# Mixture-of-experts stage of a two-layer decoder: gathered tokens turned on TensorE, or by strip transfers and VectorE's 32 by 32 transposes

## Chip, cores and metric

One core of one Trainium2 chip runs the whole program. The metric is device time in microseconds (us), lower is better. The kernel before takes 2111.92 us, the median of 3 runs (2110.97 to 2113.27).

## What is computed

Two decoder layers over 8 sequences of 256 tokens with 512 features, everything in float32: differential attention, a long convolution, a mixture of experts (MoE), local attention, cross attention and a gated attention, with a residual and a layer norm behind each. Only the MoE matters here. Every token picks 2 of 8 experts, and the stage computes for each pick

```
h = silu(x @ gate[e]) * (x @ up[e])      # x: 512 features, h: 352
y = h @ down[e]                          # y: 512 features
```

The two results are then weighted by the router's shares and summed.

## The kernel before

Stages follow each other with a barrier of all engines between them: front, long convolution, middle (layer norm, router, sorting of the picks into tiles), experts, tail. The middle stage sorts the 4096 picks by expert into `TILES` = 39 tiles of 128 tokens, one expert each, and keeps for each tile its list of tokens (`tokens`) and its expert (`tile_expert`).

`experts_stage` (from L1593) handles the tiles in order, s = 0 to 38. For each tile:

- GpSimd (L1620) gathers 128 rows of x from HBM into `xg[s % 2]` by an indirect DMA, once TensorE has turned the tile that lay there.
- TensorE turns the rows (`turn_x`, L1634): four 128x128 transposes into one PSUM bank, `xT_ps`. VectorE copies the bank to SBUF as `xT` (L1716). Features now lie on partitions.
- TensorE computes gate and up (`project`, L1639), four matmuls each, into `gu_ps`. ScalarE takes silu of gate (L1690), VectorE multiplies by up (L1721), TensorE turns the hidden rows (L1658), ScalarE copies them (L1705, L1707), and TensorE multiplies by the down matrix (`moe_y_ps`, L1667).
- VectorE copies y to SBUF (L1733), and ScalarE's queue stores it in HBM (L1694).

The order of TensorE's work is written out by hand: gate of tile s+1, turn of the hidden rows of s, up of s+1, turn of x of s+2, down of s. The expert of a tile is a number in SBUF, which TensorE's sequencer reads (L1626, `TENSOR_LOAD`) behind the semaphore waits and ahead of the matmuls. VectorE's order in each step is product of s+1, copy of the turned x of s+2, copy of y of s. SyncE (SP) has nothing to do in this stage. ScalarE's queue issues at the start a 1 MB load, `early_wq`, which the tail uses.

The tail turns some of its own blocks another way (`turn_strips`, L188, and `shift_strips`, L194): VectorE's transposes turn each 32 by 32 block in its place, and 16 DMAs, one for each pair of a source strip of 32 partitions and a target strip, carry the blocks to their partitions. In each such DMA 32 partitions send 8 runs of 32 floats:

```
eng.dma_start(out.rearrange("p c (t q) -> p (c t) q", q=P)[lanes, :, rows],
              blocks.rearrange("p (n k) -> p n k", k=P)[rows, :, lanes]).then_inc(done, 16)
```

Of the kernel before, what the change touches and what calls it, by code (L numbers as in the profile page):

```python
# [193 lines left out]
def shift_strips(eng, out, blocks, done):  # L194


    for s in range(4):
        for k in range(4):
            lanes, rows = slice(32 * k, 32 * k + 32), slice(32 * s, 32 * s + 32)
            eng.dma_start(out.rearrange("p c (t q) -> p (c t) q", q=P)[lanes, :, rows],  # L200
                          blocks.rearrange("p (n k) -> p n k", k=P)[rows, :, lanes]).then_inc(done, 16)


def project_cols(pe, out, w, xT, col, n=P):
# [965 lines left out]
def ctx_stores(b):  # L1170

    return sum(2 if n >= EARLY else 1 for n in range(b % 2, b, 2))
# [420 lines left out]
def experts_stage(nc, consts, mid, region, x_in, y_slots, early, early_loaded, w_tail):  # L1593


    with ExitStack() as ctx:
        st = Stage(nc, ctx, "moe")
        at = AT_SMALL + 320 + 4 * D
        xT = mid.xT
        hT = region.at("moe_hT", at + 2048, [P, 3, P])  # L1600
        y = [region.at(f"moe_y{p}", at + 3584 + 2048 * p, [P, D]) for p in range(2)]
        silu = region.at("moe_silu", AT_CTX + 2 * KB4, [P, 2, HID])
        hid = region.at("moe_hid", AT_CTX + 2 * KB4 + 2816, [P, 2, HID])
        xg, wgu, wd, gathered = mid.xg, mid.gu, mid.down, mid.gathered
        gu_ps = st.ps("gu_ps", [P, 2, 2, 512])
        xT_ps = st.ps("xT_ps", [P, 512])
        hT_ps = st.ps("hT_ps", [P, 512])
        y_ps = st.ps("y_ps", [P, 2, 512])
        y_stored = mid.y_stored
        sem = {n: st.sem(n) for n in (  # L1610
            "x_turned", "xT_taken", "gate_ready", "up_ready", "silu_ready", "hid_ready", "h_turned", "hT_taken", "y_ready", "y_taken")}

        with nc.Block() as block:
            @block.gpsimd
            def _(pool):
                for s in range(2, TILES):
                    p = s % 2
                    if s > 2:
                        pool.wait_ge(sem["x_turned"], s - 2)
                    pool.indirect_dma_start(out=xg[p][:], out_offset=None, in_=x_in,  # L1620
                                            in_offset=bass.IndirectOffsetOnAxis(ap=mid.tokens[:, s:s + 1], axis=0)).then_inc(gathered[p], 16)

            @block.tensor
            def _(pe):
                def expert(s):
                    return pe.value_load(mid.tile_expert[0:1, s:s + 1], min_val=0, max_val=E_ - 1)  # L1626

                def turn_x(s):
                    p = s % 2
                    pe.wait_ge(gathered[p], 16 * (s // 2) + 16)  # L1630
                    if s > 1:
                        pe.wait_ge(sem["xT_taken"], s - 1)
                    for c in range(NC):
                        ins = pe.transpose(xT_ps[:, c * P:(c + 1) * P], xg[p][:, c * P:(c + 1) * P], consts["ident"][:])  # L1634
                    ins.then_inc(sem["x_turned"], 1)

                def project(s, h, e):
                    for c in range(NC):
                        ins = pe.matmul(gu_ps[:, s % 2, h, 0:HID], (xT if s else mid.xT_first)[:, c, :], wgu[c][:, e, h * HID:(h + 1) * HID],  # L1639
                                        start=c == 0, stop=c == NC - 1)  # L1640
                    return ins

                def gate(s):
                    if s:
                        pe.wait_ge(sem["xT_taken"], s)
                    if s >= 2:
                        pe.wait_ge(sem["hid_ready"], s - 1)
                    project(s, 0, expert(s)).then_inc(sem["gate_ready"], 1)

                def up(s):  # L1650
                    project(s, 1, expert(s)).then_inc(sem["up_ready"], 1)

                def turn_hid(s):
                    pe.wait_ge(sem["hid_ready"], s + 1)
                    if s:
                        pe.wait_ge(sem["hT_taken"], s)
                    for n, (lo, w) in enumerate(HC):
                        ins = pe.transpose(hT_ps[0:w, n * P:(n + 1) * P], hid[:, s % 2, lo:lo + w], consts["ident"][:])  # L1658
                    ins.then_inc(sem["h_turned"], 1)

                def down(s):
                    e = expert(s)
                    pe.wait_ge(sem["hT_taken"], s + 1)
                    if s >= 2:
                        pe.wait_ge(sem["y_taken"], s - 1)
                    for n, (lo, w) in enumerate(HC):
                        ins = pe.matmul(y_ps[:, s % 2, :], hT[0:w, n, :], wd[n][0:w, e, :], start=n == 0, stop=n == 2)  # L1667
                    ins.then_inc(sem["y_ready"], 1)

                pe.wait_ge(mid.first_half, 16 * 7)  # L1670
                gate(0)
                turn_x(1)
                up(0)
                for s in range(TILES):
                    if s + 1 == HALVES[1][0]:
                        pe.wait_ge(mid.second_half, 16 * 6)
                    if s + 1 < TILES:
                        gate(s + 1)
                    turn_hid(s)
                    if s + 1 < TILES:  # L1680
                        up(s + 1)
                    if s + 2 < TILES:
                        turn_x(s + 2)
                    down(s)

            @block.scalar
            def _(act):
                def swish(s):
                    act.wait_ge(sem["gate_ready"], s + 1)
                    act.activation(silu[:, s % 2, :], gu_ps[:, s % 2, 0, 0:HID], ACT.Silu).then_inc(sem["silu_ready"], 1)  # L1690

                def store(s):
                    act.wait_ge(sem["y_taken"], s + 1)
                    act.dma_start(y_slots[s * P:(s + 1) * P, :], y[s % 2][:]).then_inc(y_stored[s % 2], 16)  # L1694

                for p in range(2):
                    act.wait_ge(mid.ctx_stored[p], 16 * ctx_stores(B - 2 + p))
                for k in early:
                    act.dma_start(early[k][:], w_tail[k].rearrange("(c p) e -> p c e", p=P)).then_inc(early_loaded[k], 16)
                swish(0)  # L1700
                for s in range(TILES):
                    if s + 1 < TILES:
                        swish(s + 1)
                    act.wait_ge(sem["h_turned"], s + 1)
                    act.copy(hT[:, 0:2, :], hT_ps[:, 0:2 * P].rearrange("p (k n) -> p k n", n=P))  # L1705
                    w = HC[2][1]
                    act.copy(hT[0:w, 2, :], hT_ps[0:w, 2 * P:3 * P]).then_inc(sem["hT_taken"], 1)  # L1707
                    if s:
                        store(s - 1)
                store(TILES - 1)  # L1710

            @block.vector
            def _(dve):
                def take_x(s):
                    dve.wait_ge(sem["x_turned"], s)
                    dve.tensor_copy(xT[:], xT_ps[:].rearrange("p (c n) -> p c n", n=P)).then_inc(sem["xT_taken"], 1)  # L1716

                def product(s):
                    dve.wait_ge(sem["silu_ready"], s + 1)
                    dve.wait_ge(sem["up_ready"], s + 1)  # L1720
                    dve.tensor_tensor(hid[:, s % 2, :], gu_ps[:, s % 2, 1, 0:HID], silu[:, s % 2, :], ALU.mult).then_inc(sem["hid_ready"], 1)  # L1721

                take_x(1)
                product(0)
                for s in range(TILES):
                    if s + 1 < TILES:
                        product(s + 1)
                    if s + 2 < TILES:
                        take_x(s + 2)
                    dve.wait_ge(sem["y_ready"], s + 1)  # L1730
                    if s >= 2:
                        dve.wait_ge(y_stored[s % 2], 16 * (s // 2))
                    dve.tensor_copy(y[s % 2][:], y_ps[:, s % 2, :]).then_inc(sem["y_taken"], 1)  # L1733


def tail_stage(nc, consts, region, y_stored, x_in, x_out, y_slots, slot, share, ctx_q, ctx_o, wa, wvo, w, early, early_loaded, cT, ctx_wq, ctx_wo):
# [5 lines left out]
    with ExitStack() as ctx:  # L1742
# [124 lines left out]
        with nc.Block() as block:  # L1867
# [412 lines left out]
            def _(sp):  # L2280
# [17 lines left out]
                def shift(k, b, key):  # L2298
                    sp.wait_ge(blocks_made[k], blocks_count(k, b))
                    sp.wait_ge(ring.filled_sem(key), ring.count(key))  # L2300
                    shift_strips(sp, xT[b % 2][:], blocks_of(k), xT_loaded[b % 2])

                for r in range(B + 3):
                    if 2 <= r < B:
# [736 lines left out]
```

## Time and profile before

| What | Value |
|---|---|
| Median of 3 runs | 2111.92 us |
| Profiled execution | 2113.61 us |
| Its span | 2111.7 us |
| TensorE matmuls busy | 2041.3 us (97%) |
| VectorE busy | 1146.7 us (54%) |
| ScalarE, GpSimd busy | 500.7 us, 579.5 us |
| Granted TensorE clock, mean | 0.993 of full speed |

A row of the trace names the line of the program, the engine, the operation and the tiles (out<-in). PE is TensorE's matmuls, PEld its weight loads, DVE VectorE, ACT ScalarE, POOL GpSimd, and SPq, ACTq and POOLq are the queues on which SyncE, ScalarE and GpSimd issue DMAs. A float32 matmul has two records, so four matmuls show as x8; a transpose has one. Duration of a matmul is longer than the distance to the next, since they are pipelined: distances are taken from start to start.

### The profile page before, as it was taken

The page shows a single profiled execution, that of the slowest core. Times are in us where ns is not written, and L with a number is a line of the kernel's source. Part 1 is how long each engine was busy: PE and PEld are TensorE (multiplying, and loading weights), DVE is VectorE, ACT ScalarE, POOL GpSimd, SP SyncE. Part 2 cuts the span into 40 slices and gives each one's busy share as a digit, 9 for nine tenths or more (in the row PEclk, how much of TensorE's full clock was granted, in tenths as well). Part 3 has the DMA queues.
Part 4 walks back from the last instruction along what each step waited for, and adds up shares of the span by engine and source line. Part 5 has one row for each costly group of instructions (what it writes and reads, how often), then busy time and mean ns, then how long its engine had stood idle before and what let it go on. Part 6 is the DMA issues. An engine that isn't in the chain of part 4 may idle for free. (4 is left out here: it accounts for less than half of the span.)

```text
span 2111.7 us, 32316 instructions
## 1 busy us (share of the span) xinstructions
PE 2041.3 (97%) x13303; PEld 1180.7 (56%) x13303; DVE 1146.7 (54%) x1748; ACT 500.7 (24%) x757; POOL 579.5 (27%) x548
## 2 busy tenths in 40 slices
PE   7899999999999999999999999999999999999996
PEld 5444444334444467556565665656666666666664
DVE  2567777576777764122222234365757474736567
ACT  2445444440000131111111122112222222222211
POOL 2122222228999710011111322112222212121112
PEclk9999999999999999999999999999999999999998
DMA  5101111206111146422221502302030302020000
GB/s 161 49 1 56 56 56 46 88 27 219 42 40 44 32 168 224 172 65 65 65 65 60 209 21 91 80 12 70 11 81 11 81 11 61 8 54 11 1 11 21
DMA packets 140222, 139.74 MB, mean 66 GB/s; under 512 B 80464, under 2 KB 93904, under 8 KB 140080
## 3 DMA queue, kind: packets, MB, share of 16 engines
q1 hardware_dynamic: 119952, 86.42, 13.7%
q10 hardware_dynamic: 14448, 32.64, 4.3%
q0 software_dynamic: 5680, 18.62, 3.0%
q8 instruction: 110, 1.80, 0.4%
q14 instruction: 32, 0.26, 0.0%
HBM read 97.40 MB, written 41.81 MB: 66 GB/s over the span
## 5 line engine op out<-in xcount | busy, mean ns | idle before, releaser
L1049 PE MATMUL conv_conv<-kv,toep 128*128 128x512 f32 x576 | 247.5, 593 | 0.0
L2659 DVE RECIPROCAL tail_inv<-tail_ring 128x256 f32<-128x256 f32 x63 | 110.7, 1756 | 172.4 <-PE tail_ring L1971 171.8
L1639 PE MATMUL moe_gu_ps<-gu,xT_tile 128*128 x608 | 192.4, 459 | 0.0
L1049 PEld LDWEIGHTS conv_conv<-kv,toep 128*128 128x128 f32 x576 | 109.9, 191 | 138.2 <-issue 131.0
L1083 POOL TENSOR_TENSOR kv<-vT,cT 128x512 f32<-128x512 f32 x128 | 147.1, 1173 | 16.9 <-PE conv_conv L1049 13.1
L2344 POOL TENSOR_TENSOR tail_rstd_x<-tail_rstd_x,const_minus_half 128x2 f32<-128x2 f32 x31 | 21.7, 700 | 468.4 <-DVE tail_rstd_x L2617 468.4
L1639 PEld LDWEIGHTS moe_gu_ps<-gu,xT_tile 128*128 128x128 f32 x608 | 112.5, 190 | 66.3 <-issue 17.8
L2352 POOL TENSOR_SCALAR_AFFINE_SELECT tail_expT<-tail_expT 128x1024 f32<-128x1024 f32 x64 | 71.3, 1116 | 227.6 <-ACT tail_expT L2436 227.4
L2647 DVE TENSOR_REDUCE tail_negtop<-tail_scores 128x4 f32<-128x1024 f32 x64 | 77.9, 1218 | 82.6 <-PE tail_scores L1922 82.5
L610 POOL TENSOR_SCALAR_AFFINE_SELECT front_expT<-front_expT 128x2048 f32<-128x2048 f32 x32 | 64.1, 2004 | 199.6 <-ACT front_expT L665 199.6
L1721 DVE TENSOR_TENSOR moe_hid<-moe_gu_ps,moe_silu 128x352 f32<-128x352 f32 x39 | 20.4, 524 | 170.7 <-PE moe_gu_ps L1639 170.7
L1620 POOL DMA_INDIRECT xg<-x_after,tokens x37 | 35.0, 945 | 282.2 <-PE moe_xT_ps L1634 255.1
L665 ACT ACTIVATE front_expT<-front_scores 128x2048 f32<-128x2048 f32 x48 | 90.1, 1878 | 78.2 <-PE front_scores L383 78.2
L1667 PE MATMUL moe_y_ps<-down,moe_hT 128*128 (+1 forms) x234 | 107.1, 593 | 0.7 <-ACT moe_hT L1707 0.7
L2436 ACT ACTIVATE tail_expT<-tail_scores 128x1536 f32<-128x1536 f32 x63 | 91.4, 1450 | 65.1 <-PE tail_scores L1948 65.1
L786 DVE TENSOR_REDUCE front_negtop<-front_scores 128x8 f32<-128x2048 f32 x32 | 73.2, 2288 | 22.1 <-PE front_scores L351 21.9
L1690 ACT ACTIVATE moe_silu<-moe_gu_ps 128x352 f32<-128x352 f32 x39 | 18.1, 463 | 270.3 <-PE moe_gu_ps L1639 270.3
L2357 POOL TENSOR_TENSOR tail_expT<-tail_expT 128x512 f32<-128x512 f32 x60 | 76.7, 1278 | 5.0
L1105 ACT COPY both<-conv_conv 128x512 f32<-128x512 f32 x32 | 18.6, 585 | 229.4 <-PE conv_conv L1049 212.0
L1733 DVE COPY moe_y<-moe_y_ps 128x512 f32<-128x512 f32 x39 | 27.0, 691 | 72.7 <-PE moe_y_ps L1667 72.7
L214 PE MATMUL tail_ring<-tail_gk,tail_xT 128*128 128x416 f32 (+1 forms) x256 | 63.0, 398 | 0.8 <-ACT tail_xT L2418 0.8
L1667 PEld LDWEIGHTS moe_y_ps<-down,moe_hT 128*128 128x128 f32 (+1 forms) x234 | 41.6, 191 | 38.4 <-issue 38.2
(396 smaller groups left out, 3879.9 us busy)
## 6 DMA issues: line engine op xcount, KB each, us to landing
toep<-toeplitz SPq DMA_DIRECT2D x32, 320.0 KB, 2.9
y_slots<-moe_y ACTq DMA_DIRECT2D x39, 256.0 KB, 2.0
gu<-in_L_ffn_gate_up_proj SPq DMA_DIRECT2D x5, 1408.0 KB, 12.4
toeplitz<-filt_rows SPq DMA_DIRECT2D x8, 768.0 KB
tail_xT<-tail_probs SPq DMA_DIRECT2D x176, 32.0 KB
front_e<-in_ctx SPq DMA_DIRECT2D x8, 512.0 KB, 9.7
toeplitz<-filt_rows SPq DMA_DIRECT2D x16, 256.0 KB
x_after<-x SPq DMA_DIRECT2D x8, 512.0 KB, 5.0
```

What stands on the lines that cost most here:

```text
L610: pool.affine_select(out=tile, in_=tile, compare_op=ALU.is_ge, fill=0.0, base=0, pattern=[[0, 16], [1, P]], channel_multiplier=-1).then_in ...
L665: act.activation(exp_buf(b, n)[:].rearrange("p g j q -> p g (j q)"), scores[:], ACT.Exp).then_inc(quads.drained_sem(key), 1)
L786: ins = dve.tensor_reduce(negtop[:, 1, n].rearrange("p (g a) -> p g a", a=2), scores[:].rearrange("p g (a k) -> p g a k", a=2), AX_X, ALU. ...
L1049: ins = pe.matmul(bank, toep[p][:, mat * P:(mat + 1) * P], kv[p][:, c].rearrange("p b j i -> p (b j i)"), start=n == 0, stop=n == len(PART ...
L1083: pool.tensor_tensor(kv[p][:, c], tokens_of(c, h), context_of(c, h, 3), ALU.mult).then_inc(kv_ready, 1)
L1639: ins = pe.matmul(gu_ps[:, s % 2, h, 0:HID], (xT if s else mid.xT_first)[:, c, :], wgu[c][:, e, h * HID:(h + 1) * HID], start=c == 0, stop ...
L1667: ins = pe.matmul(y_ps[:, s % 2, :], hT[0:w, n, :], wd[n][0:w, e, :], start=n == 0, stop=n == 2)
L2352: pool.affine_select(out=diagonal, in_=diagonal, compare_op=ALU.is_ge, fill=0.0, base=0, pattern=[[0, 8], [1, P]], channel_multiplier=-1). ...
L2357: pool.tensor_tensor(e[:, 3], e[:, 0], e[:, 2], ALU.add).then_inc(masked[kind], 1)
L2436: act.activation(exp_buf(kind, b, c)[:, 0:3].rearrange("p n g q -> p g n q"), quads.tile(key)[:, :, 0:3 * P].rearrange("p g (n q) -> p g n ...
L2647: dve.tensor_reduce(negtop[:, 1, heads_of(c)], scores[:, :, 0:S], AX_X, ALU.max, negate=True)
L2659: link.after(dve.reciprocal(inv[c % 2][:], bank[:, S:2 * S]))
```

## The change

The x of tiles 2 to 38 is no longer turned by TensorE. GpSimd gathers two tiles (2q and 2q+1) into one of two pair buffers. SyncE, once both have landed and VectorE has made `xT` of tile 2q-1, issues the 16 strip DMAs of `shift_strips` from the pair buffer to the one buffer `shifted`. VectorE turns the 32 by 32 blocks of one tile at a time from `shifted` into `xT[s % 2]` (`make_xT`). The copy from PSUM by VectorE and TensorE's four transposes are gone for these tiles; tile 1 keeps them. `xT` has two buffers now. The load `early_wq` moves from the stage's start to the step ahead of the last tile, since a pair buffer lies at its place. `shift_strips` itself takes flat arguments, which changes nothing for the tail.

```diff
 def shift_strips(eng, out, blocks, done):
+    to, of = (a.rearrange("p (n q) -> p n q", q=P) for a in (out, blocks))
     for s in range(4):
         for k in range(4):
             lanes, rows = slice(32 * k, 32 * k + 32), slice(32 * s, 32 * s + 32)
...
+            eng.dma_start(to[lanes, :, rows], of[rows, :, lanes]).then_inc(done, 16)
@@ experts_stage
-        xT = mid.xT
+        pairs = [region.at(f"moe_pair{n}", AT_CTX + n * KB4, [P, 2, D]) for n in range(2)]
+        shifted = region.at("moe_shifted", AT_SMALL + 320, [P, 2, D])
+        xT = [region.at("moe_xT0", AT_RAW + GU_BYTES, [P, NC, P]), region.at("moe_xT1", AT_CTX + 2 * KB4 + 5632, [P, NC, P])]
...
             @block.gpsimd
             def _(pool):
                 for s in range(2, TILES):
-                    p = s % 2
-                    if s > 2:
-                        pool.wait_ge(sem["x_turned"], s - 2)
-                    pool.indirect_dma_start(out=xg[p][:], out_offset=None, in_=x_in,
+                    q, t = s // 2, s % 2
+                    if q < 3 and t == 0:
+                        pool.wait_ge(mid.ctx_stored[q - 1], 16 * ctx_stores(B - 3 + q))
+                    elif t == 0:
+                        pool.wait_ge(sem["x_shifted"], 256 * (q - 2))
+                    pool.indirect_dma_start(out=pairs[(q - 1) % 2][:, t], out_offset=None, in_=x_in,
...
+            @block.sync
+            def _(sp):
+                for q in range(1, PAIRS + 1):
+                    tiles = range(2 * q, min(2 * q + 2, TILES))
+                    sp.wait_ge(paired[q % 2], 16 * sum(1 for s in range(2, tiles[-1] + 1) if s // 2 % 2 == q % 2))
+                    sp.wait_ge(sem["xT_made"], 2 * q - 1)
+                    shift_strips(sp, shifted[:, 0:len(tiles)].rearrange("p t d -> p (t d)"),
+                                 pairs[(q - 1) % 2][:, 0:len(tiles)].rearrange("p t d -> p (t d)"), sem["x_shifted"])
...
                 def gate(s):
                     if s:
-                        pe.wait_ge(sem["xT_taken"], s)
+                        pe.wait_ge(sem["xT_made"], s)
...
                     if s + 1 < TILES:
                         up(s + 1)
-                    if s + 2 < TILES:
-                        turn_x(s + 2)
                     down(s)
...
-                for k in early:
-                    act.dma_start(early[k][:], w_tail[k].rearrange("(c p) e -> p c e", p=P)).then_inc(early_loaded[k], 16)
                 swish(0)
                 for s in range(TILES):
                     if s + 1 < TILES:
                         swish(s + 1)
+                    if s + 2 == TILES:
+                        act.wait_ge(sem["x_shifted"], 256 * PAIRS)
+                        for k in early:
+                            act.dma_start(early[k][:], w_tail[k].rearrange("(c p) e -> p c e", p=P)).then_inc(early_loaded[k], 16)
...
             @block.vector
             def _(dve):
-                def take_x(s):
-                    dve.wait_ge(sem["x_turned"], s)
-                    dve.tensor_copy(xT[:], xT_ps[:].rearrange("p (c n) -> p c n", n=P)).then_inc(sem["xT_taken"], 1)
+                def make_xT(s):
+                    dve.wait_ge(sem["x_shifted"], 256 * (s // 2))
+                    if s > 2:
+                        dve.wait_ge(sem["up_ready"], s - 1)
+                    dve.transpose(xT[s % 2][:].rearrange("p c n -> p (c n)"), shifted[:, s % 2]).then_inc(sem["xT_made"], 1)
...
-                take_x(1)
+                dve.wait_ge(mid.ctx_stored[1], 16 * ctx_stores(B - 1))
+                dve.wait_ge(sem["x_turned"], 1)
+                dve.tensor_copy(xT[1][:], xT_ps[:].rearrange("p (c n) -> p c n", n=P)).then_inc(sem["xT_made"], 1)
```

The order of instructions on TensorE, ahead of the down matmuls of one tile and the gate of the next. Before:

```order
 L1639 MATMUL moe_gu_ps<-gu_67,xT_tile 128x352
 L1634 MATMUL moe_xT_ps<-const_ident,xg_75 128x128 [waits moe_xT_taken,mid_gathered0]
 L1634 MATMUL moe_xT_ps<-const_ident,xg_75 128x128 x3
 L1626 TENSOR_LOAD tile_expert
 L1626 ISA x2
 L1667 ISA [waits moe_y_taken,moe_hT_taken]
 L1667 MATMUL moe_y_ps<-down_68,moe_hT 128x512
```

With the change, from the down matmuls to the next gate:

```order
 L1642 TENSOR_LOAD tile_expert
 L1642 ISA x2
 L1680 ISA [waits moe_y_taken,moe_hT_taken]
 L1680 MATMUL moe_y_ps<-down_68,moe_hT 128x512
 L1680 REGISTER_ALU
 L1680 MATMUL moe_y_ps<-down_69,moe_hT 128x512
 L1680 REGISTER_ALU
 L1680 MATMUL moe_y_ps<-down_70,moe_hT 128x512
 L1642 TENSOR_LOAD tile_expert [waits moe_hid_ready,moe_xT_made]
 L1642 ISA x2
 L1652 ISA
 L1652 MATMUL moe_gu_ps<-gu_64,moe_xT_7468 128x352
```

The four transposes between up and down are gone, and the gate's read of the expert's number stands behind a wait for `xT_made`.

On SyncE's queue, behind the stage's barrier, where there was nothing before (two of the 19 pairs):

```order
 L1630 UNCONDITIONAL_BRANCH [waits barrier_Pool_Activation_PE_DVE_SP_release]
 L201 DMA moe_shifted<-moe_pair_7464 32x8x32 [waits moe_xT_made,moe_paired1]
 L201 DMA moe_shifted<-moe_pair_7464 32x8x32 x15
 L201 DMA moe_shifted<-moe_pair_7465 32x8x32 [waits moe_xT_made,moe_paired0]
 L201 DMA moe_shifted<-moe_pair_7465 32x8x32 x15
```

And on VectorE, in the steady state:

```order
 L1736 TENSOR_TENSOR moe_hid<-moe_gu_ps,moe_silu 128x352 [waits moe_up_ready,moe_silu_ready]
 L1731 STREAM_TRANSPOSE moe_xT_7468<-moe_shifted 128x512 [waits moe_up_ready,moe_x_shifted]
 L1750 COPY moe_y_7470<-moe_y_ps 128x512 [waits mid_y_stored0,moe_y_ready]
 L1736 TENSOR_TENSOR moe_hid<-moe_gu_ps,moe_silu 128x352 [waits moe_up_ready,moe_silu_ready]
 L1731 STREAM_TRANSPOSE moe_xT_7467<-moe_shifted 128x512 [waits moe_up_ready,moe_x_shifted]
```

The 32x8x32 DMAs are new on SyncE, 16 for each pair behind a wait for `xT_made`; on VectorE the transpose has the place of the copy `xT_tile<-moe_xT_ps`, behind the product and ahead of the copy of y.

## Rows read from the trace of the kernel before

**Rows 1.** The page: span, busy time, and its 40 slices.
```profile
span 2111.7 us, 32316 instructions
PE 2041.3 (97%) x13303; PEld 1180.7 (56%) x13303; DVE 1146.7 (54%) x1748; ACT 500.7 (24%) x757; POOL 579.5 (27%) x548
...
PE   7899999999999999999999999999999999999996
```

**Rows 2.** Stretches: us, busy PE, PEld, DVE, ACT, POOL; clock, DMA share, GB/s.
```profile
859.00:1180.00 321.00, 316.94 (x1127) 189.62 (x1127) 70.17 (x116) 35.94 (x118) 34.96 (x37) 0.99 0.21 69
1010.44:1018.52 8.08, 8.08 (x30) 4.85 (x29) 1.81 (x3) 0.89 (x3) 0.94 (x1) 1.00 0.21 67
```

**Rows 3.** Timeline of one tile, TensorE and VectorE: start, us, what.
```profile
1002.36 0.60 PE L1634 MATMUL moe_xT_ps<-const_ident,xg 128*128 128x128 f32 x4
...
1002.63 0.52 DVE L1721 TENSOR_TENSOR moe_hid<-moe_gu_ps,moe_silu 128x352 f32<-128x352 f32 x1 [4.44 <-PE moe_gu_ps L1639]
...
1002.80 2.74 PE L1667 MATMUL moe_y_ps<-down,moe_hT 128*128 x6
1003.07 0.68 DVE L1716 COPY xT_tile<-moe_xT_ps 128x512 f32<-128x512 f32 x1
...
1005.38 2.53 PE L1639 MATMUL moe_gu_ps<-gu,xT_tile 128*128 x8
...
1007.75 0.49 PE L1658 MATMUL moe_hT_ps<-const_ident,moe_hid 128*128 128x128 f32 x3
...
1008.07 2.53 PE L1639 MATMUL moe_gu_ps<-gu,xT_tile 128*128 x8
...
1010.44 0.60 PE L1634 MATMUL moe_xT_ps<-const_ident,xg 128*128 128x128 f32 x4
```

**Rows 4.** The instructions on the tile moe_xT_ps (ns min/median/max).
```profile
L1634 PE MATMUL moe_xT_ps<-const_ident,xg x152: 272/273/273, 865.2 to 1164.3; 128*128 128x128 f32 x152
```

**Rows 5.** Timeline of SyncE's queue in the tail: trains of 16 strip DMAs.
```profile
1336.18 10.98 SPq L200 DMA_DIRECT2D tail_xT<-tail_probs  x16
1351.30 10.38 SPq L200 DMA_DIRECT2D tail_xT<-tail_probT  x16
...
1538.39 11.78 SPq L200 DMA_DIRECT2D tail_xT<-tail_probs  x16
...
1884.44 11.28 SPq L200 DMA_DIRECT2D tail_xT<-tail_probT  x16
```

**Rows 6.** The tile tail_xT: its strip DMAs, ns to issue one.
```profile
L200 SPq DMA_DIRECT2D tail_xT<-tail_probs x176: 585/611/1607, 1336.2 to 1874.5; - x176
```

**Rows 7.** Stretches around the train of 1351.30 (last two numbers: DMA share, GB/s).
```profile
1351.30:1352.30 1.00, 1.00 (x3) 0.38 (x2) 0.00 (x0) 0.54 (x1) 0.00 (x0) 1.00 0.00 0
1352.30:1361.50 9.20, 9.20 (x41) 5.37 (x40) 0.00 (x0) 1.17 (x2) 0.00 (x0) 1.00 0.31 50
...
1362.40:1362.70 0.30, 0.30 (x13) 0.18 (x6) 0.00 (x0) 0.00 (x0) 0.00 (x0) 1.00 0.56 90
1362.70:1363.00 0.30, 0.30 (x2) 0.27 (x3) 0.28 (x1) 0.00 (x0) 0.00 (x0) 1.00 0.00 0
```

**Rows 8.** Line L191: VectorE's transposes in the tail.
```profile
L191 DVE STREAM_TRANSPOSE tail_probs<-tail_x x11: 1233/1245/1245, 1334.9 to 1862.5; 128x1024 f32<-128x1024 f32 x11
```

**Rows 9.** Line L1626: what TensorE's sequencer does for an expert's number.
```profile
L1626 PEldq TENSOR_LOAD <-tile_expert x117: 295/302/1499, 859.1 to 1172.9; - x117
L1626 PEldq FUSED_REGOPS  x117: 151/151/165, 860.6 to 1173.3; - x117
```

**Rows 10.** Timeline at the start of the stage: TensorE, VectorE, ScalarE's wait.
```profile
861.03 4.32 PE L1639 MATMUL moe_gu_ps<-gu,xT_first 128*128 x8 [4.00 <-issue]
...
864.78 1.28 ACT L1690 ACT_TABLE_LOAD   x1 [7.12 <-DMA ctx_o<-ctxo]
...
865.19 0.60 PE L1634 MATMUL moe_xT_ps<-const_ident,xg 128*128 128x128 f32 x4
...
865.83 0.69 DVE L1716 COPY xT_tile<-moe_xT_ps 128x512 f32<-128x512 f32 x1 [14.93 <-PE moe_xT_ps L1634]
```

**Rows 11.** Stretches with idle TensorE ahead of work at a low clock.
```profile
393.00:396.80 3.80, 0.00 (x0) 0.00 (x0) 3.53 (x5) 1.02 (x1) 2.55 (x2) 1.00 0.73 245
396.80:400.20 3.40, 3.18 (x4) 1.31 (x5) 0.00 (x0) 0.00 (x0) 0.00 (x0) 0.58 0.28 106
...
857.00:861.00 4.00, 0.04 (x1) 0.00 (x0) 0.00 (x0) 0.59 (x1) 0.94 (x1) 1.00 0.56 136
861.00:864.50 3.50, 3.47 (x7) 2.10 (x8) 0.00 (x0) 0.00 (x0) 0.00 (x0) 0.58 0.88 299
```

**Rows 12.** The page: DMA issues, KB each, us to landing.
```profile
y_slots<-moe_y ACTq DMA_DIRECT2D x39, 256.0 KB, 2.0
...
early_wq<-in_L_attn_w_qkv ACTq DMA_DIRECT2D x1, 1024.0 KB, 5.3
...
xg<-x_after,tokens POOLq DMA_INDIRECT x39, 3.3
```

More of the change, by code:

```diff
@@ L199, in shift_strips @@
             lanes, rows = slice(32 * k, 32 * k + 32), slice(32 * s, 32 * s + 32)
-            eng.dma_start(out.rearrange("p c (t q) -> p (c t) q", q=P)[lanes, :, rows],
-                          blocks.rearrange("p (n k) -> p n k", k=P)[rows, :, lanes]).then_inc(done, 16)
+            eng.dma_start(to[lanes, :, rows], of[rows, :, lanes]).then_inc(done, 16)
 def project_cols(pe, out, w, xT, col, n=P):
@@ L1610, in experts_stage @@
         sem = {n: st.sem(n) for n in (
-            "x_turned", "xT_taken", "gate_ready", "up_ready", "silu_ready", "hid_ready", "h_turned", "hT_taken", "y_ready", "y_taken")}
+            "x_turned", "x_shifted", "xT_made", "gate_ready", "up_ready", "silu_ready", "hid_ready", "h_turned", "hT_taken", "y_ready", "y_taken")}
+        paired = [st.sem(f"paired{p}") for p in range(2)]
+        PAIRS = (TILES - 1) // 2
         with nc.Block() as block:
@@ L1616, in _ @@
                 for s in range(2, TILES):
-                    p = s % 2
-                    if s > 2:
-                        pool.wait_ge(sem["x_turned"], s - 2)
-                    pool.indirect_dma_start(out=xg[p][:], out_offset=None, in_=x_in,
-                                            in_offset=bass.IndirectOffsetOnAxis(ap=mid.tokens[:, s:s + 1], axis=0)).then_inc(gathered[p], 16)
+                    q, t = s // 2, s % 2
[4 more added lines that the diff above has]
+                    pool.indirect_dma_start(out=pairs[(q - 1) % 2][:, t], out_offset=None, in_=x_in,
+                                            in_offset=bass.IndirectOffsetOnAxis(ap=mid.tokens[:, s:s + 1], axis=0)).then_inc(paired[q % 2], 16)
+            @block.sync
[6 more added lines that the diff above has]
+                                 pairs[(q - 1) % 2][:, 0:len(tiles)].rearrange("p t d -> p (t d)"), sem["x_shifted"])
             @block.tensor
@@ L1626, in expert, with turn_second @@
                     return pe.value_load(mid.tile_expert[0:1, s:s + 1], min_val=0, max_val=E_ - 1)
[L1628 to L1632, printed above, removed]
+                def turn_second():
+                    pe.wait_ge(gathered[1], 16)
                     for c in range(NC):
-                        ins = pe.transpose(xT_ps[:, c * P:(c + 1) * P], xg[p][:, c * P:(c + 1) * P], consts["ident"][:])
+                        ins = pe.transpose(xT_ps[:, c * P:(c + 1) * P], xg[1][:, c * P:(c + 1) * P], consts["ident"][:])
                     ins.then_inc(sem["x_turned"], 1)
@@ L1638, in project @@
                     for c in range(NC):
-                        ins = pe.matmul(gu_ps[:, s % 2, h, 0:HID], (xT if s else mid.xT_first)[:, c, :], wgu[c][:, e, h * HID:(h + 1) * HID],
+                        ins = pe.matmul(gu_ps[:, s % 2, h, 0:HID], (xT[s % 2] if s else mid.xT_first)[:, c, :], wgu[c][:, e, h * HID:(h + 1) * HID],
                                         start=c == 0, stop=c == NC - 1)
@@ L1671, in _ @@
                 gate(0)
-                turn_x(1)
+                turn_second()
                 up(0)
@@ L1728, in _ @@
                     if s + 2 < TILES:
-                        take_x(s + 2)
+                        make_xT(s + 2)
                     dve.wait_ge(sem["y_ready"], s + 1)
@@ L2300, in shift @@
                     sp.wait_ge(ring.filled_sem(key), ring.count(key))
-                    shift_strips(sp, xT[b % 2][:], blocks_of(k), xT_loaded[b % 2])
+                    shift_strips(sp, xT[b % 2][:].rearrange("p c s -> p (c s)"), blocks_of(k), xT_loaded[b % 2])
                 for r in range(B + 3):
```

## Prediction

> **What bounds the kernel now.** I read the page first, then the stage's own stretch, then one tile's timeline. TensorE is busy 97% of the span [rows 1], so any other engine matters only where TensorE waits for it. The experts' stage is the stretch from 859 to 1180 us: 316.94 of 321.00 us of it are matmuls, at a clock of 0.99 [rows 2]. Inside, a tile takes 8.08 us with 8.08 us of TensorE busy [rows 2]; no engine and no DMA is waited for. The period can be read off the starts in [rows 3]: turn of x 0.44 us (1002.36 to 1002.80), down 2.58, gate 2.37, turn of the hidden rows 0.32, up 2.37, sum 8.08. Whatever leaves TensorE shortens the program one for one, and whatever TensorE then waits for lengthens it.
>
> **What the change removes.** There are 152 transposes in 38 turns [rows 4]; one turn stays. 37 x 0.44 = **16.3 us** leave TensorE. VectorE loses 37 copies of 0.68 us [rows 3] and gets 37 transposes of 128x512. The tail's transposes of 128x1024 take 1.245 us [rows 8], so half of that, 0.62 us, is my estimate; by the nearest copy it would be 0.68. In either case VectorE has room (1.81 us busy of 8.08 [rows 2]).
>
> **What it adds: a serial loop through SyncE.** `shifted` has one buffer. The 16 strip DMAs of pair q start only when `xT` of tile 2q-1 is made, and `xT` of tile 2q needs all 16 to have landed. TensorE works meanwhile, but only on what it already has. So I compare two paths, both from T, the end of up of tile 2q-2 (1002.36 in [rows 3]), to the first gate matmul of tile 2q.
>
> TensorE's own work: down 2.58, gate of 2q-1 2.37, turn of hidden rows 0.32, up of 2q-1 2.37, down 2.58 = **10.22 us**.
>
> The loop:
> - Product starts at T+0.27 and takes 0.52 [rows 3]; the transpose of tile 2q-1 follows: xT made at T+1.4.
> - SyncE issues 16 DMAs. The same helper with the same shape (32 partitions x 8 runs of 128 bytes, 32 KB) runs in the tail 17 times: the trains take 10.38 to 11.78 us, mean 11.0 [rows 5], and one issue takes 0.611 us in the median, 0.585 at least [rows 6]. It is the queue's issuing that takes the time, not the moving: while the train of 1351.30 runs, the DMA engines are 0.31 busy at 50 GB/s [rows 7]. I take 11.0, since one store of y falls in each train here, as loads do in some of the tail's.
> - Landing: that train's last issue ended at 1361.68, and the DMA share falls to nothing at 1362.70 [rows 7]: 1.0 us, with semaphores 1.2.
> - Transpose of tile 2q: 0.6.
> - TensorE's sequencer was waiting, so its read of the expert's number is no longer covered by running matmuls: 0.30 + 0.15 [rows 9], some register work and the first weights. The read took 1.5 us the one time it stood behind a barrier [rows 9]. Bounds 0.4 and 1.9; I take 0.9, near the median read.
>
> Sum 1.4 + 11.0 + 1.2 + 0.6 + 0.9 = 15.1 us, against 10.22: TensorE **waits 4.9 us in every pair**. After it the pair goes on with gate, turn and up, and the next loop starts; nothing makes up for the wait, because each train begins behind the one before's last reader. The first pair is the same: its train waits for the copy of tile 1 (from 865.83 [rows 10]), 13.7 us ahead of gate 2, which TensorE could start at 875.6.
>
> There are 19 trains, 18 of full size: 18 x 4.9 = **88.2 us**. The last carries one tile, 16 DMAs of half the bytes: no row shows such an issue; between a full train (4.9) and a wait of 0, I take 2.
>
> **The clock.** An idle TensorE is followed by a low clock in this trace. After 3.80 us without a matmul the clock of the next 3.40 us was 0.58, after 4.00 us idle it was 0.58 for 3.50 us [rows 11], that is at the lower level, 1.2 GHz. The gate that followed took 4.16 us (861.03 to 865.19 [rows 10]) in place of 2.37: 1.8 us lost. A wait of 4.9 us is longer than both. Part of a low stretch may fall into the wait itself, where it costs nothing, so bounds 0 and 1.8 us for each wait; I take 1.3, nearer the upper, which both rows show: 19 x 1.3 = **24.7 us**.
>
> **What is hidden.** The indirect gathers stay as many, 0.94 us each on GpSimd, and land in 3.3 [rows 12]; a pair buffer is free when its own train has landed, a whole pair ahead. The y copy of tile 2q-2 now waits behind VectorE's blocked transpose, some 2 us later than before, but its bank is wanted again only after two more gates. VectorE's new wait for a context store ends when ScalarE's did, at 864.78, ahead of the turn it waits for at 865.19 [rows 10]. `early_wq` lands in 5.3 us [rows 12] with the last tile's up and two downs still to come: nothing.
>
> **Sum**, against the profiled execution: 2113.6 - 16.3 + 88.2 + 2 + 24.7 = 2212.2. That execution is 1.7 us over the median, so **2210.5 us**, 98.6 more than 2111.9. A measurement of this kernel can tell about 0.2%, 4 us.
>
> **A rule against the rows.** The sum prices a transfer by the time its queue takes to issue it [rows 5, 6]. The Trainium skill ("DMA: Bandwidth & Descriptors", section "Issuing engines are not separate DMA queues") says the opposite of what decides here: the sequencer's time to initiate a DMA is usually small relative to the DMA itself. By its fit of 2.0 us plus bytes over 436 GB/s, 512 KB would be shifted in some 3.2 us (an estimate from that page). The trace disagrees: 0.61 us of issue for each 32 KB. Were it so here, rival 1 would hold.
>
> **Rivals.**
> 1. *The trains hide and the change is faster.* TensorE waits for nothing if the train takes less than 10.22 - 1.4 - 1.2 - 0.6 - 0.9 = 6.1 us, that is 0.38 us for each issue. Then 2111.9 - 16.3 = 2095.6 us. For it: SyncE has nothing else in this stage, while in the tail it has loads beside. Against it: all 17 trains are above 10.3 us, quiet ones too, and the shortest of 176 issues was 0.585 us [rows 6]. 4%.
> 2. *The waits are there, the clock stays up.* The low stretches fall in the waits, or do not come. 2210.5 - 24.7 = 2185.8 us. For it: nothing in the rows says that a low stretch must begin only when TensorE resumes. Against: in both places of [rows 11] it did. 22%.
> 3. *The trains are longer here*, since y stores and gathers run beside them, or the expert's read takes 1.5 us each time. One issue took 1.607 us at most [rows 6]. With trains of 11.8, the read at its upper bound and the full clock loss, each wait is 6.7 + 1.8 us: 2111.9 - 16.3 + 18 x 8.5 + 6.7 = 2255 us, and beyond where trains pass 12 us. 8%.
>
> My forecast has 66%: waits near 4.9 with some clock loss, 2190 to 2245. **Range:** with trains of 10.4 us and the read at 0.4 a wait is 3.8, and without any clock loss that gives 2111.9 - 16.3 + 18 x 3.8 = 2164. I take 2165 to 2248, which leaves out rival 1, most of rival 3 and a little of the forecast's edges. **Chances:** slower by over 0.2% 0.95 (the forecast, rivals 2 and 3, short of a point for a train just short enough), faster 0.04, within 0.2% 0.01.
>
> **What would show it.** On SyncE's queue in this stage: 19 trains of 16, each near 11 us, starting some 0.05 us after a VectorE transpose of an odd tile. In TensorE's waits: 19 on the gate, near 4.9 us each, released by VectorE's transpose; pair period near 21 us instead of 16.2. Odd tiles' gates should wait for nothing. TensorE's clock in the stage below 0.99, with gates of even tiles near 3.7 us rather than 2.4. Transposes near 0.62 us. Wrong would be: trains under 6 us (rival 1), or a wait whose releaser is the gather or a y store.

## The result and the profile after

| | Before | Changed |
|---|---|---|
| Median | 2112.18 us (4 runs) | 2230.86 us (4 runs, 2228.03 to 2233.34) |
| Ratio | 1 | 1.0558, 95% interval 1.0543 to 1.0573 |
| Span of the profiled execution | 2111.7 us | 2225.6 us |
| Mean granted clock | 0.993 | 0.971 |

The change costs 118.7 us, 5.6%. The forecast was 2210.5 us in a range of 2165 to 2248.

The page of the changed kernel, against [rows 1] (the clock's row stands here too):

```profile
span 2225.6 us, 32343 instructions
...
PE 2070.6 (93%) x13155; PEld 1188.7 (53%) x13155; DVE 1148.3 (52%) x1748; ACT 502.0 (23%) x757; POOL 579.4 (26%) x548
...
PE   7899999999999998787878799999999999999996
...
PEclk9999999999999998888888899999999999999998
```

TensorE has fewer instructions (148 transposes are gone) and yet more busy time, and its share and its clock both fall in the slices of the experts' stage. The tail is untouched: from its first matmul (1294.46) to the end it takes 931.1 us, as before (from 1180.65, 931.0 us). The profiled execution reached the stage's first gate 6.2 us sooner (854.85 against 861.03 [rows 10]), in stages that the change leaves alone. So its span is 113.9 us longer, while the stage itself takes 120.0 us more. Two of the four runs of the changed kernel lie at 2228 us and two at 2233, and what makes this difference is not shown.

TensorE's waits in the stage (engine, line, released by: us in total, times, longest):

```profile
PE moe_gu_ps L1652 <- DVE moe_xT L1731: 82.0, 18, 5.3
PE moe_gu_ps L1652 <- issue: 8.2, 2, 4.4
```

The second row is one wait of the same kind (4.4 us) and the 3.8 us ahead of the stage's first gate, which stood there before as 4.0 [rows 10]. So the change adds 19 waits, 86.4 us, 4.55 each, all on a gate, all behind VectorE's transpose. Such a row counts from the end of the matmul before, which lies 0.16 us behind the start that the next one could have had (a down takes 2.74 us as a duration and 2.58 from start to start). So a wait costs 0.16 us more than listed: 4.71 in the mean, 89.5 us in all. What VectorE and SyncE waited for:

```profile
DVE moe_xT L1731 <- DMA moe_shifted<-moe_pair: 94.1, 19, 5.8
...
SPq L1635 <- DVE moe_xT L1731: 210.6, 18, 12.4
```

The loop can be read from these: TensorE waits for VectorE, VectorE for the strip transfers, and SyncE for VectorE's transpose of the tile before. Its pieces, from the timeline and from the rows of the tile `moe_shifted`:

```profile
997.16 10.40 SPq L201 DMA_DIRECT2D moe_shifted<-moe_pair  x16
...
1264.53 10.61 SPq L201 DMA_DIRECT2D moe_shifted<-moe_pair  x16
...
L201 SPq DMA_DIRECT2D moe_shifted<-moe_pair x304: 585/611/1605, 861.5 to 1274.5; - x152
L1731 DVE STREAM_TRANSPOSE moe_xT<-moe_shifted x37: 700/711/714, 874.0 to 1276.4; 128x512 f32<-128x512 f32 x37
...
DMA to landing us min/median/max: 1.8/1.9/3.2
```

Twelve of the 19 trains take 10.4 us, the others up to 11.4, and the mean is 10.6. An issue takes 0.611 us, as in the tail [rows 6]. The train at 1264.53 is the last, which moves one tile: half the bytes, and it takes no less. One pair on TensorE and VectorE:

```profile
1003.32 2.74 PE L1680 MATMUL moe_y_ps<-down,moe_hT 128*128 x6
1003.59 0.53 DVE L1736 TENSOR_TENSOR moe_hid<-moe_gu_ps,moe_silu 128x352 f32<-128x352 f32 x1 [4.44 <-PE moe_gu_ps L1652]
1008.87 0.71 DVE L1731 STREAM_TRANSPOSE moe_xT<-moe_shifted 128x512 f32<-128x512 f32 x1 [4.75 <-DMA moe_shifted<-moe_pair]
...
1010.39 4.32 PE L1652 MATMUL moe_gu_ps<-gu,moe_xT 128*128 x8 [4.34 <-DVE moe_xT L1731]
1014.55 0.49 PE L1671 MATMUL moe_hT_ps<-const_ident,moe_hid 128*128 128x128 f32 x3
...
1017.25 2.74 PE L1680 MATMUL moe_y_ps<-down,moe_hT 128*128 x6
1017.52 0.52 DVE L1736 TENSOR_TENSOR moe_hid<-moe_gu_ps,moe_silu 128x352 f32<-128x352 f32 x1 [7.36 <-PE moe_gu_ps L1652]
1017.96 0.70 DVE L1731 STREAM_TRANSPOSE moe_xT<-moe_shifted 128x512 f32<-128x512 f32 x1
1019.83 2.53 PE L1652 MATMUL moe_gu_ps<-gu,moe_xT 128*128 x8
```

The gate of the even tile starts 4.49 us late, counted from where down's 2.58 us end (1005.90), and then takes 4.16 us (1010.39 to 1014.55) instead of 2.37. The gate of the odd tile waits for nothing. This is the milder case: in 8 of the 19 even tiles the gate takes 3.9 to 4.2 us, in the other 11 it takes 4.85, and there the low clock reaches into the turn of the hidden rows, as behind the first and the last wait:

```profile
875.53 5.05 PE L1652 MATMUL moe_gu_ps<-gu,moe_xT 128*128 x8 [4.89 <-DVE moe_xT L1731]
880.38 0.73 PE L1671 MATMUL moe_hT_ps<-const_ident,moe_hid 128*128 128x128 f32 x3
...
1277.96 5.06 PE L1652 MATMUL moe_gu_ps<-gu,moe_xT 128*128 x8 [4.53 <-DVE moe_xT L1731]
1282.81 0.85 PE L1671 MATMUL moe_hT_ps<-const_ident,moe_hid 128*128 128x128 f32 x3
```

From 875.53 to 1277.96 there are 18 pairs: 22.36 us each, where two tiles took 16.16 before. The stretches of the pair above (us; busy PE, PEld, DVE, ACT, POOL; clock, DMA share, GB/s):

```profile
1005.90:1010.39 4.49, 0.16 (x1) 0.00 (x1) 1.29 (x2) 0.00 (x0) 0.98 (x2) 1.00 0.18 29
1010.39:1014.55 4.16, 4.16 (x8) 2.39 (x9) 0.00 (x0) 0.00 (x0) 0.91 (x1) 0.59 0.47 126
1014.55:1026.00 11.45, 11.45 (x40) 6.88 (x39) 2.36 (x4) 1.77 (x6) 0.00 (x0) 1.00 0.30 74
```

While TensorE waits, the DMA engines are 0.18 busy. The wait is a chain, one link after the other: SyncE still issues its last DMAs (to 1007.56, 1.7 us), they land (1.3 us, to 1008.87), VectorE transposes (0.7 us), TensorE starts (0.8 us).

Where the low clock begins differs between the two cases. The first wait, with its long stretch, and the wait of 1010.39, with a short one:

```profile
871.00:874.00 3.00, 0.00 (x0) 0.00 (x0) 0.00 (x0) 0.00 (x0) 0.00 (x0) 1.00 0.28 45
874.00:875.53 1.53, 0.00 (x1) 0.01 (x1) 1.29 (x2) 0.00 (x0) 0.95 (x2) 0.51 0.00 0
875.53:880.80 5.27, 5.27 (x10) 3.16 (x11) 0.00 (x0) 0.18 (x1) 0.93 (x1) 0.50 0.34 100
880.80:881.80 1.00, 1.00 (x5) 0.71 (x4) 0.00 (x0) 0.82 (x3) 0.00 (x0) 0.98 0.00 0
...
1010.40:1013.80 3.40, 3.40 (x6) 2.03 (x7) 0.00 (x0) 0.00 (x0) 0.90 (x1) 0.52 0.57 154
1013.80:1014.60 0.80, 0.80 (x4) 0.39 (x3) 0.00 (x0) 0.00 (x0) 0.00 (x0) 0.89 0.00 0
```

The short stretch lasts 3.4 us and costs 1.8 us. The long one begins in the wait, 1.5 us ahead of the gate, and lasts 6.8 us, so that 5.3 us of work still run at the lower level, which costs 2.7 us here (2.48 on the gate, 0.24 on the turn of the hidden rows). A pair of 22.36 us is 15.28 of work (16.16 less 0.88 for two turns), 4.71 of wait, and 2.37 for the low clock, the mean of both cases.

### The profile page after: what moved, and what is told of

Its sections match the earlier page's. It is cut to its first block and busy times, and to the rows that moved or that the text cites. A ratio compares the mean times of both kernels' runs of the same rounds, so it can differ in the third digit from the quotient of the medians.

```text
span 2225.6 us, 32343 instructions
## 1 busy us (share of the span) xinstructions
PE 2070.6 (93%) x13155; PEld 1188.7 (53%) x13155; DVE 1148.3 (52%) x1748; ACT 502.0 (23%) x757; POOL 579.4 (26%) x548
## 5 line engine op out<-in xcount | busy, mean ns | idle before, releaser
L1652 PE MATMUL moe_gu_ps<-gu,moe_xT 128*128 x608 | 235.4, 539 | 86.4 <-DVE moe_xT L1731 82.0
L1652 PEld LDWEIGHTS moe_gu_ps<-gu,moe_xT 128*128 128x128 f32 x608 | 131.6, 226 | 175.5 <-issue 138.7
L1627 POOL DMA_INDIRECT moe_pair<-x_after,tokens x37 | 34.9, 944 | 371.8 <-DMA moe_shifted<-moe_pair 336.3
L1731 DVE STREAM_TRANSPOSE moe_xT<-moe_shifted 128x512 f32<-128x512 f32 x37 | 26.1, 707 | 94.1 <-DMA moe_shifted<-moe_pair 94.1
```

The lines of the kernel that those rows point to most:

```text
L1652: ins = pe.matmul(gu_ps[:, s % 2, h, 0:HID], (xT[s % 2] if s else mid.xT_first)[:, c, :], wgu[c][:, e, h * HID:(h + 1) * HID], start=c == ...
```

## Experiments

Theory A: the train of 16 issues on one queue, with a single `shifted` buffer that makes it serial, sets the pace, and the low clock behind each wait is a second cost of it. Rivals: the small transfers are slow as such or fight over the DMA engines (B); an issue costs by what it moves (C); the slow gate has a reason other than the idle time before it.

### Two buffers for the shifted blocks

```diff
-        shifted = region.at("moe_shifted", AT_SMALL + 320, [P, 2, D])
+        shifted = [region.at(f"moe_shifted{p}", AT_SMALL + 320 + 4096 * p, [P, 2, D]) for p in range(2)]
...
-                    sp.wait_ge(sem["xT_made"], 2 * q - 1)
+                    sp.wait_ge(sem["xT_made"], max(1, 2 * q - 3))
```

Completion is counted on a semaphore for each buffer, since two trains may be in flight. To make room, the product of silu and up is written over silu, and `hT`, `y` and `xT` are placed anew.

> The changed kernel with two buffers for shifted blocks, so that SyncE issues the train of a pair while VectorE still reads the pair before. Theory A (the waits come from a serial loop: issue train of 10.4 us, landing, transpose, all behind the last reader of the one buffer): trains stay at 10.4 us, but 10.4 is less than the 15.3 us of TensorE's work for a pair, so all but the first wait vanish, the clock stays at 1.0, and the time is 2112.2 - 16.3 = 2096 us, plus up to 7 for the first pair: 2096 to 2103. Theory B (strip transfers are too slow as such, by descriptors of 128 bytes and contention on the DMA engines): waits remain or trains grow once they overlap with gathers and stores; time stays above 2150.

Measured: 2104.93 us, ratio 0.9958 (0.9945 to 0.9972). All of TensorE's waits for x in the stage, and the strip DMAs:

```profile
PE moe_gu_ps L1655 <- DVE moe_xT L1735: 4.2, 1, 4.2
...
L201 SPq DMA_DIRECT2D moe_shifted<-moe_pair x304: 585/611/1967, 864.9 to 1142.3; - x152
...
DMA to landing us min/median/max: 1.8/2.0/4.1
```

The time is 2 us above the expected range, but the waits are gone as theory A says: the same 304 DMAs at the same 0.611 us now cost one wait instead of 19. The transfers overlap with gathers and stores, and land in 2.0 us. Theory B falls: neither the size of the runs nor contention was the trouble, but that each train began only behind the last reader of the one buffer.

### Useless matmuls in the wait

```diff
                 def gate(s):
+                    if s >= 2 and s % 2 == 0:
+                        for n in range(5):
+                            pe.matmul(xT_ps[:], consts["ident"][:], wgu[0][:, 0, 0:512], start=True, stop=True)
```

> The changed kernel with five useless 512-column matmuls on TensorE (4.3 us) ahead of the wait for xT of each even tile; their results are thrown away. Theory A with the clock as a second cost: the waits shrink from 4.6 us to some 0.3, the loop is not longer, the clock stays at 1.0 and the gates of even tiles take 2.4 us instead of 4.8; 19 x 2.5 = 48 us come back, time about 2183 us, with more work done. Rival (the gate is slow for another reason than the idle time before it, for instance SBUF or DMA contention): time unchanged at 2231, gates of even tiles still 4.8 us. If the loop were not the limit, 19 x 4.3 = 82 us would be added: 2312.

Measured: 2190.53 us, ratio 1.0367 (1.0352 to 1.0383), 40.3 us less than the changed kernel, with 95 more matmuls. The timeline around one pair:

```profile
1003.12 2.63 PE L1653 MATMUL moe_gu_ps<-gu,moe_xT 128*128 x8 [0.48 <-issue]
1005.58 0.49 PE L1675 MATMUL moe_hT_ps<-const_ident,moe_hid 128*128 128x128 f32 x3
...
1018.50 4.46 PE L1660 MATMUL moe_xT_ps<-gu,const_ident 128*128 128x512 f32 x10
1022.98 1.45 PE L1653 MATMUL moe_gu_ps<-gu,moe_xT 128*128 x4
```

The even gate takes 2.46 us (1003.12 to 1005.58), and this pair 19.86 us (to 1022.98). Over 18 pairs (first fill 877.99, last 1240.48) the mean is 20.14 us instead of 22.36, 2.22 less. The fills with what is left of the waits take 4.86 us in each pair, 0.15 more than the waits that they replace, so the low clock had cost 2.37. So the slow gate came from the idle time before it. That the time lies 7 us above the expected 2183 fits in the main: the low clock had cost 19 x 2.37 = 45 us, not 48, and the longer fills take back 3.

### The expert's number read ahead of the wait

```diff
+                    e = expert(s)
                     if s:
                         pe.wait_ge(sem["xT_made"], s)
...
-                    project(s, 0, expert(s)).then_inc(sem["gate_ready"], 1)
+                    project(s, 0, e).then_inc(sem["gate_ready"], 1)
```

> The changed kernel with TensorE's sequencer reading the expert's number ahead of the wait for xT, not behind it. Theory A (the read, 0.30 + 0.15 us and its checks, is exposed at the end of each wait): each of 19 waits is 0.45 to 0.5 us shorter, time 2221 to 2223 us. Rival (the time from VectorE's transpose to the first matmul, 0.8 us, is semaphore and weight load): no change, 2231.

Measured: 2215.35 us, ratio 1.0488 (1.0472 to 1.0504), 15.5 us less than the changed kernel:

```profile
PE moe_gu_ps L1652 <- DVE moe_xT L1732: 74.2, 19, 5.0
```

The 19 waits sum to 74.2 us instead of 86.4, 0.64 us less each, so the read was exposed, somewhat more than the two rows of [rows 9] say. The rest of the gain is not in the waits, and the two traces show where it comes from: here 6 of the 19 even gates take 4.85 us, in the changed kernel 11. A pair takes 21.44 us in the mean (873.93 to 1259.85), 0.92 less than there; the waits are 0.61 of it, and the other 0.31, 5.6 us over 18 pairs, is low clock. Together with the 12.2 us of the waits this is nearly all of the 18.0 us between the two profiled spans. Behind shorter waits the long stretches came less often; why is not shown.

### The train split over two queues

SyncE issues the 8 DMAs of source strips 0 and 1, ScalarE, behind the same two waits, those of strips 2 and 3, ahead of the silu of the next tile:

```diff
+                    if s % 2 == 0 and s + 2 < TILES:
+                        second_half(s // 2 + 1)
                     if s + 1 < TILES:
                         swish(s + 1)
```

> The changed kernel with the 16 strip DMAs of a pair split: 8 on SyncE's queue, 8 on ScalarE's, both behind the same waits. Theory A (each queue's own issuing sets the train, 0.65 us apiece): trains of 5.2 us, the loop falls to 9.8 us, under TensorE's 10.2, waits and low clock vanish. ScalarE is taken for 5.2 us, so its copy of the hidden rows may come up to 0.4 us late in each pair: 2096 to 2106 us. Theory B (the two queues share what makes a descriptor, or the DMA engines are the limit): each half takes as long as the whole did, 10 us, ScalarE is held for it and silu comes late too: 2231 us or more.

Measured: 2113.41 us, ratio 1.0003 (0.9994 to 1.0013). The queues of SyncE and ScalarE in one pair, the DMAs' rows, and TensorE's waits:

```profile
999.89 5.18 SPq L201 DMA_DIRECT2D moe_shifted<-moe_pair  x8
...
999.91 5.51 ACTq L201 DMA_DIRECT2D moe_shifted<-moe_pair  x8
...
L201 SPq DMA_DIRECT2D moe_shifted<-moe_pair x152: 585/612/2067, 870.4 to 1165.3; - x152
L201 ACTq DMA_DIRECT2D moe_shifted<-moe_pair x152: 592/639/1765, 870.4 to 1165.6; - x152
...
PE moe_y_ps L1680 <- ACT moe_hT L1729: 11.2, 20, 1.7
...
890.13 2.53 PE L1652 MATMUL moe_gu_ps<-gu,moe_xT 128*128 x8
892.98 2.84 PE L1680 MATMUL moe_y_ps<-down,moe_hT 128*128 x6 [0.31 <-ACT moe_hT L1729]
895.65 1.64 PE L1652 MATMUL moe_gu_ps<-gu,moe_xT 128*128 x5
```

Both queues issue side by side, each at its own 0.61 to 0.64 us: the train is halved, one buffer is enough, and no gate waits any more. The time is 7 us above the upper end of what I expected, and in the profile most of it is there: ScalarE, held for 5.5 us, copies the hidden rows late, and TensorE waits 11.2 us for them in place of 0.7. From start to start each of these waits costs some 0.26 us more than listed (890.13 to 895.65 is 5.52 us, up and down take 4.95, the row says 0.31), so they cost 0.8 us a pair where I had allowed 0.4, 15.4 us in all. That is nearly the whole gain of the removed turns, and the time is that of the kernel before. None of these waits, at most 1.7 us long, is followed by a low clock.

### One train for each tile

```diff
-                    sp.wait_ge(sem["xT_made"], 2 * q - 1)
-                    shift_strips(sp, shifted[:, 0:len(tiles)].rearrange("p t d -> p (t d)"),
-                                 pairs[(q - 1) % 2][:, 0:len(tiles)].rearrange("p t d -> p (t d)"), sem["x_shifted"])
+                    for s in tiles:
+                        sp.wait_ge(sem["xT_made"], max(1, s - 2))
+                        shift_strips(sp, shifted[:, s % 2], pairs[(q - 1) % 2][:, s % 2], landed[s % 2])
```

> The changed kernel with one train of 16 DMAs for each tile (128 runs of 128 bytes a DMA) instead of one for a pair (256 runs), each half of the shifted buffer being refilled on its own, so that a train overlaps with the use of the other half. Theory A (an issue costs the same 0.65 us whatever it moves): SyncE is busy 10.4 us for each tile, more than TensorE's 7.64, so it sets the pace: 37 x 10.5 = 388 us in place of 37 x 7.64, and the clock, low or not, costs nothing since TensorE waits anyway: about 2112.2 - 16.3 + 37 x 2.8 = 2200 us. Theory C (an issue costs by its descriptors or bytes): trains of 5.2 us for each tile, hidden, 2096 to 2105 us.

Measured: 2210.24 us, ratio 1.0464 (1.0448 to 1.048).

```profile
L201 SPq DMA_DIRECT2D moe_shifted<-moe_pair x592: 585/601/1594, 866.4 to 1257.3; - x198
...
PE moe_gu_ps L1654 <- DVE moe_xT L1734: 72.6, 32, 4.8
```

A DMA of half the runs and half the bytes takes 0.601 us to issue against 0.611. Theory C falls for these strip DMAs. From 866.4 to 1257.3 the 592 issues come every 0.66 us, 10.6 us for a tile on which TensorE has 7.64 us of work: the queue never rests and sets the pace. 37 x (10.6 - 7.64) = 110 us over 2096 give 2206, near the 2210.

That does not make the price of an issue the same for every DMA. The store of y moves 256 KB, eight times a strip DMA of a pair, and in the kernel before it takes about half the time to issue:

```profile
L1694 ACTq DMA_DIRECT2D y_slots<-moe_y x39: 326/327/327, 879.0 to 1179.4; - x39
```

What in a strip DMA makes its issue dearer is not shown: no run changes the length of its runs.

### Two buffers, and the first pair turned by TensorE

Two buffers, and tiles 2 and 3 turned by TensorE as tile 1 is, so that the first train runs under their work:

```diff
-                for q in range(1, PAIRS + 1):
+                for q in range(2, PAIRS + 1):
...
                         up(s + 1)
+                    if s < 2:
+                        turn_x(s + 2)
                     down(s)
```

> The kernel of two buffers, with tiles 2 and 3 turned by TensorE as tile 1 is, so that the strip transfers begin with tile 4. Theory A: the one wait left in that kernel (4.2 us on the gate of tile 2) and the low clock behind it (2.5 us) go, two turns (0.9 us) come back: 5.8 us less than 2104.9, about 2099 us. Rival: the wait only moves to the gate of tile 4, and nothing is gained: 2105 us.

Measured: 2096.78 us (5 runs), ratio 0.9924 (0.991 to 0.9937): 0.76% faster than the kernel before, where the version with two buffers alone gained 0.42%. No wait for x is left in the stage; what TensorE waits for there is the start and the last copy of the hidden rows, as before:

```profile
PE moe_gu_ps L1662 <- issue: 3.8, 1, 3.8
...
PE moe_y_ps L1690 <- ACT moe_hT L1733: 0.7, 1, 0.7
```

## Why the prediction was right, and where it was too small

- **Turns removed, 16.3 us.** Right, but seen only where the loop is out of the way: with 35 of the 37 turns gone and no wait, 15.6 us come back (2112.39 to 2096.78) where 35 x 0.44 = 15.4.
- **The loop, 15.1 us against 10.22, a wait of 4.9.** Right in kind and in size: 4.55 as listed, 4.71 from start to start. The terms were off by little and both ways. The trains take 10.6 us in the mean, not 11.0. Landing takes 1.3 us in the pair shown (1007.56 to 1008.87), taken as 1.2. The transpose takes 0.71 us, not 0.6: half of the duration for 1024 columns was too little. The start of TensorE took 0.8 us (transpose's end at 1009.58 to 1010.39), taken as 0.9.
- **The last train, 2 us between 0 and 4.9.** The upper end was right (4.53 as listed): an issue costs the same for half the bytes, as the train of 1264.53 and the run with a train for each tile both show. All 19 waits cost 89.5 us, where 88.2 + 2 = 90.2 were forecast.
- **The clock, 1.3 us for each wait within 0 and 1.8.** This is the term that was too small. It measures 2.37, beyond my upper bound: 22.36 less 15.28 of work and 4.71 of wait, and the run with useless matmuls gives the same. The bound came from the one gate of [rows 10] that followed 4.0 us of idle time, with a low stretch of 3.5 us. Behind 11 of the 19 waits the stretch was twice as long. Part of the stretch did fall into the wait, as I had allowed, but that saved nothing: the stretches that begin there are the long ones, and they cost the most. 19 x 2.37 = 45 us against the 24.7 of the forecast: this is the whole of the miss of 20.4 us. Sum: -16.3 + 89.5 + 45 = 118 us, measured 118.7.
- **That the range held is in part luck.** The terms of the waits were nearly exact, but the bound on the clock was too low. With its 1.8 the forecast would have been some 2220 us; the range's upper end of 2248 took the measured 2231 in because it left room for longer trains, which did not come.
- **Hidden work.** As said: no wait on gathers, y stores or `early_wq`, and the tail starts as before.
- **Rivals.** The trains hid (rival 1) only with a second buffer or a second queue. The clock did not stay up (rival 2). The trains were not longer here (rival 3), yet the time came out between the forecast and that rival, through the clock. The rule weighed against the rows does not fit this case: 0.61 us of issue for each DMA decides here, a third of the 1.9 us from issue to landing, and in a train of 16 the issues add up while the landings overlap. So the Trainium skill's "usually small relative to the DMA itself" does not hold for transfers of 32 KB in trains of 16. The fit quoted beside it stands in another section of that page ("Anatomy of one DMA — SWDGE (gpsimd) path") and is for DMAs on GpSimd's path, while these are SyncE's. The section of the rule ("DMA: Bandwidth & Descriptors", "Issuing engines are not separate DMA queues") also says that a second issuing engine saves the sequencer's time, and the split train shows just that.

## What to carry to other kernels

Before moving work from a full engine to DMAs, count the issues and read what one of that shape takes (0.61 us for a strip DMA, 0.33 for the larger store of y), and lay the chain of one round (issue train, landing, next engine, restart of the waiting one) beside the full engine's work in the same round: with one buffer the chain must fit wholly, with two only its longest link. Here the waits of 4.3 to 5.3 us on TensorE were paid twice, once as idle time and once as the low clock behind it, and the second part was half of the first. Where the loop was not shortened, even useless matmuls in its wait gave the second part back.

## What the runs showed of the hardware that was not expected

- Halving what a strip DMA moves hardly changes its issue: 0.611 us for 32 KB in 256 runs, 0.601 us in the kernel where all carry 16 KB in 128 runs. The store of y, 256 KB, takes 0.327 us.
- Two queues issue side by side without slowing each other much: 8 DMAs in 5.18 us on SyncE's while ScalarE's took 5.51 for its 8.
- Behind each of the 19 waits of 4.3 to 5.3 us the clock was at the lower level, in two lengths: 3.4 to 3.6 us behind 8 of them (0.52 from 1010.40 to 1013.80) and 6.8 to 7.0 us behind 11 (0.51 from 874.00, 0.50 to 880.80), which begin up to 1.5 us ahead of the gate. In the trace before no low stretch with TensorE at work is longer than 3.6 us. What decides between the two lengths is not shown.
- Waits of 0.2 to 1.7 us, 20 of them in the kernel with the train split over two queues, left the clock up.
- 95 useless matmuls made the kernel 40 us faster.
